# A transformer block's two layer norms: the inverse root as a power on GpSimd instead of a square root on ScalarE

## The reference

```
def _layernorm(x, axis=-1, eps=1e-05):
    m = jnp.mean(x, axis=axis, keepdims=True)
    v = jnp.var(x, axis=axis, keepdims=True)
    return (x - m) / jnp.sqrt(v + eps)

h = emb_weight[ids] + (lora_A[:, ids].T @ lora_B.T) * 2
h = h + attention(_layernorm(h))      # 16 heads of 16, window of 64 to each side, plus 64 global keys, gated
h = h + experts(_layernorm(h))        # 8 experts, 256 -> 1024 -> 256, the best 2 per token, capacity 1.25
```

## Time and profile before

| | us |
|---|---|
| timed runs | 3863.5, 3874.36, 3875.84 (median 3874.36) |
| span of the profiled execution, first to last instruction | 3869.2 |
| busy: TensorE, GpSimd, VectorE, ScalarE | 3468.8, 2331.8, 2237.8, 1988.5 |

### The profile page before, as it was taken

The page is one execution under the profiler, slowest core; times in us unless marked ns, Lnnn a source line. Parts: engine busy times, 40 slices in busy tenths (PEclk is TensorE's granted clock), DMA queues, the critical chain, the costliest instruction groups (busy, mean ns, idle before and its releaser), DMA issues. The chain is left out here.

```text
span 3869.2 us, 118995 instructions
## 1 busy us (share of the span) xinstructions
PE 3468.8 (90%) x47729; PEld 2822.7 (73%) x47730; DVE 2237.8 (58%) x5391; ACT 1988.5 (51%) x3119; POOL 2331.8 (60%) x2664
## 2 busy tenths in 40 slices
PE   3889898889998989988998759999999998999998
PEld 1566565656565656565655559999999998999998
DVE  3577777777777687777786433434333433343333
ACT  0566666666665666666666434444444444444343
POOL 5467768677777777777776544444444444444443
PEclk7899999999999999999999879999999999999999
DMA  4445445444544444444444132333333333222222
GB/s 138 128 149 150 139 129 158 130 151 132 154 135 147 133 146 142 146 138 150 140 149 131 55 98 46 66 49 59 57 57 58 59 56 67 47 50 45 44 45 40
DMA packets 242497, 397.77 MB, mean 103 GB/s; under 512 B 34572, under 2 KB 150748, under 8 KB 242044
## 3 DMA queue, kind: packets, MB, share of 16 engines
q1 hardware_dynamic: 168540, 297.43, 24.8%
q0 software_dynamic: 70512, 91.16, 13.6%
q10 hardware_dynamic: 3008, 2.95, 0.2%
HBM read 198.55 MB, written 192.88 MB: 101 GB/s over the span
## 5 line engine op out<-in xcount | busy, mean ns | idle before, releaser
L1349 POOL DMA_INDIRECT out_y<-out_t,tok_out x264 | 425.2, 1611 | 766.5 <-DMA out_y<-out_t,tok_out 390.3
L1495 ACT ACTIVATE act<-psS 128x512 f32<-128x512 f32 x528 | 316.2, 599 | 907.8 <-PE psS L1423 907.8
L1557 DVE TENSOR_TENSOR h_lo<-act,h_hi 128x512 fp32r<-128x512 f32 x528 | 367.1, 695 | 586.6 <-ACT h_hi L1496 586.6
L879 ACT ACTIVATE pl<-psS 128x896 f32<-128x896 f32 x512 | 468.5, 915 | 291.5 <-PE psS L727 285.0
L1458 PE MATMUL psO<-w_hi,h_hi 128*128 128x256 f32 x2112 | 598.5, 283 | 0.0
L1458 PE MATMUL psO<-w_lo,h_hi 128*128 128x256 f32 x2112 | 588.6, 279 | 0.0
L1458 PE MATMUL psO<-w_hi,h_lo 128*128 128x256 f32 x2112 | 587.6, 278 | 0.0
L556 POOL TENSOR_SCALAR_AFFINE_SELECT pl<-pl 128x512 f32<-128x512 f32 x512 | 353.3, 690 | 376.9 <-ACT pl L879 375.9
L1423 PE MATMUL psS<-xg_hi,w_hi 128*128 128x256 f32 x1984 | 551.8, 278 | 0.0
L1423 PE MATMUL psS<-xg_hi,w_lo 128*128 128x256 f32 x1984 | 551.5, 278 | 0.0
L1423 PE MATMUL psS<-xg_lo,w_hi 128*128 128x256 f32 x1984 | 551.4, 278 | 0.0
(11 more groups left out here) (233 smaller groups left out, 7780.4 us busy)
## 6 DMA issues: line engine op xcount, KB each, us to landing
qk_scr<-qk SPq DMA_DIRECT2D x64, 768.0 KB, 4.2
Q<-qk_scr SPq DMA_DIRECT2D x128, 384.0 KB, 4.5
K<-qk_scr SPq DMA_DIRECT2D x128, 384.0 KB, 5.3
qk_scr<-qk SPq DMA_DIRECT2D x64, 512.0 KB, 3.4
qk_scr<-qk SPq DMA_DIRECT2D x64, 256.0 KB, 3.4
h_rows<-held SPq DMA_DIRECT2D x32, 512.0 KB
hb<-h_rows SPq DMA_DIRECT2D x32, 512.0 KB
out_y<-h SPq DMA_DIRECT2D x32, 512.0 KB
```

What stands on the lines that cost most here:

```text
L879: act.activation(pl[:, v, half, :, lo:hi], psS[:, 0:2, lo:hi], ACT.Exp, scale=SCALE).then_inc(exp_done, 1)
L1349: pool.indirect_dma_start(out=y[:, :], in_=out_t[:, tile.out, s, :], in_offset=None, out_offset=bass.IndirectOffsetOnAxis(ap=tok_out[:, ti ...
L1495: act.activation(act32[:, b, :, 0:cols], src, ACT.Silu)
L1557: dve.tensor_tensor(h_lo[:, 2 * b:2 * b + 2, 0:cols], act32[:, b, :, 0:cols], h_hi[:, 2 * b:2 * b + 2, 0:cols].bitcast(F32), ALU.subtract) ...
```

## The change

The square roots on ScalarE go. VectorE adds epsilon to the variances (`var1`, `var2`), and GpSimd raises the sums to the power of minus one half, with a constant tile `neg_half` as the exponent; VectorE's reciprocals go as well. The new entries stand here in the lists: on VectorE `var2` behind the second half of `stats2`, `var1` behind the second half of `stats1`; on GpSimd `rstd2` between the selects of exponentials 12 and 13, and `rstd1` behind the last `residual` and ahead of the next sequence's first select. `scale2` of block 0 moves on VectorE from before `kg` 0 to behind the maximum 4. Nothing else is moved.

```
-                    dve.memset(eps_b[:, :], EPS)
+                    dve.memset(neg_half[:, :], -0.5)
 ORDER["act"]
-                ("cur", "exp", 11), ("cur", "exp", 12), ("prev", "std2", None), ("cur", "exp", 13), ...
+                ("cur", "exp", 11), ("cur", "exp", 12), ("cur", "exp", 13), ...
-                ("far", "std1", None), ("cur", "exp", 19), ...
+                ("cur", "exp", 19), ...
 ORDER["dve"]
-                ("nxt", "rstd1", None), ("cur", "cut", (1, 0)), ...
+                ("cur", "cut", (1, 0)), ...
-                ("far", "lora", 0), ("nxt", "max", 3), ("prev", "rstd2", None), ("prev", "scale2", 0), ("nxt", "kg", 0),
-                ("far", "lora", 1), ("nxt", "max", 4), ("prev", "scale2", 1), ...
+                ("prev", "var2", None), ("far", "lora", 0), ("nxt", "max", 3), ("nxt", "kg", 0),
+                ("far", "lora", 1), ("nxt", "max", 4), ("prev", "scale2", 0), ("prev", "scale2", 1), ...
-                ("nxt", "max", 8), ("far", "stats1", 1), ("nxt", "max", 9),
+                ("nxt", "max", 8), ("far", "stats1", 1), ("far", "var1", None), ("nxt", "max", 9),
 ORDER["pool"]
-                ("old", "scatter", 4), ("cur", "sel", 12), ("cur", "sel", 13), ("next", "gather", 0), ...
+                ("old", "scatter", 4), ("cur", "sel", 12), ("prev", "rstd2", None), ("cur", "sel", 13), ("next", "gather", 0), ...
-                ("cur", "sel", 18), ("prev", "residual", 2), ("prev", "residual", 3), ("nxt", "sel", 0), ...
+                ("cur", "sel", 18), ("prev", "residual", 2), ("prev", "residual", 3), ("far", "rstd1", None), ("nxt", "sel", 0), ...
 GpSimd
+                        if stage == "rstd1":
+                            pool.wait_ge(var1_done, s + 1)
+                            pool.tensor_tensor(rstd1[:, :], var1[:, :], neg_half[:, :], ALU.pow).then_inc(rstd1_done, 1)
 ScalarE
-                        if stage == "std1":
-                            act.wait_ge(mv1_done, s + 1)
-                            act.activation(std1[:, :], mv1[:, :, 1], ACT.Sqrt, bias=eps_b[:, :]).then_inc(std1_done, 1)
 VectorE
-                        if stage == "rstd1":
-                            dve.wait_ge(std1_done, s + 1)
-                            dve.reciprocal(rstd1[:, :], std1[:, :]).then_inc(rstd1_done, 1)
+                        if stage == "var1":
+                            dve.wait_ge(mv1_done, s + 1)
+                            dve.tensor_scalar(var1[:, :], mv1[:, :, 1], EPS, None, ALU.add).then_inc(var1_done, 1)
```

More of the change, by code:

```diff
@@ L144, in build @@
         neg_bg = keep("neg_bg", [P, 1])
-        eps_b = keep("eps_b", [P, 1])
+        neg_half = keep("neg_half", [P, QB])
         iota8 = keep("iota8", [P, E])
@@ L481, in build @@
                 ("cur", "exp", 9), ("far", "embed", None), ("cur", "exp", 10), ("cur", "evac", (1, 0)), ("nxt", "gate", None),
-                ("cur", "exp", 11), ("cur", "exp", 12), ("prev", "std2", None), ("cur", "exp", 13), ("cur", "evac", (1, 1)),
+                ("cur", "exp", 11), ("cur", "exp", 12), ("cur", "exp", 13), ("cur", "evac", (1, 1)),
                 ("cur", "exp", 14), ("cur", "exp", 15), ("nxt", "m_rows", 0), ("cur", "exp", 16), ("prev", "x2_t", 0),
                 ("prev", "x2_t", 1), ("cur", "exp", 17), ("cur", "exp", 18), ("cur", "evac", (2, 0)), ("cur", "evac", (2, 1)),
-                ("far", "std1", None), ("cur", "exp", 19), ("nxt", "values", 0), ("nxt", "values", 1), ("nxt", "m_rows", 1),
+                ("cur", "exp", 19), ("nxt", "values", 0), ("nxt", "values", 1), ("nxt", "m_rows", 1),
                 ("nxt", "values", 2), ("far", "xn_t", 0), ("far", "xn_t", 1), ("far", "qk", 0), ("nxt", "exp", 0),
@@ L489, in build @@
             ORDER["dve"] = (
-                ("nxt", "rstd1", None), ("cur", "cut", (1, 0)), ("cur", "kg", 1), ("cur", "cut", (1, 1)), ("old", "rank", 3),
+                ("cur", "cut", (1, 0)), ("cur", "kg", 1), ("cur", "cut", (1, 1)), ("old", "rank", 3),
                 ("nxt", "scale1", 0), ("cur", "cut", (1, 2)), ("cur", "gate1", None), ("cur", "kg", 2), ("cur", "cut", (1, 3)),
@@ L511, in build @@
                 ("cur", "sel", 8), ("nxt", "hold", 1), ("nxt", "hold", 2), ("nxt", "hold", 3), ("cur", "sel", 10), ("cur", "sel", 11),
-                ("old", "scatter", 4), ("cur", "sel", 12), ("cur", "sel", 13), ("next", "gather", 0), ("next", "gather", 1),
+                ("old", "scatter", 4), ("cur", "sel", 12), ("prev", "rstd2", None), ("cur", "sel", 13), ("next", "gather", 0), ("next", "gather", 1),
                 ("next", "gather", 2), ("old", "scatter", 5), ("old", "scatter", 6), ("old", "scatter", 7), ("cur", "sel", 15),
                 ("prev", "residual", 0), ("cur", "sel", 16), ("cur", "sel", 17), ("next", "gather", 3), ("prev", "residual", 1),
-                ("cur", "sel", 18), ("prev", "residual", 2), ("prev", "residual", 3), ("nxt", "sel", 0), ("far", "qk3", 0),
+                ("cur", "sel", 18), ("prev", "residual", 2), ("prev", "residual", 3), ("far", "rstd1", None), ("nxt", "sel", 0), ("far", "qk3", 0),
                 ("far", "qk3", 1), ("past", "scatter", 0), ("far", "qk3", 2), ("far", "qk3", 3), ("nxt", "sel", 1), ("nxt", "sel", 2),
@@ L596, in _ @@
                             pool.tensor_tensor(qk3[:, arg, :], qk_rest[:, arg, :], qk2[:, arg, :], ALU.subtract).then_inc(qk3_done, 1)
+                        if stage == "rstd1":
+                            pool.wait_ge(var1_done, s + 1)
+                            pool.tensor_tensor(rstd1[:, :], var1[:, :], neg_half[:, :], ALU.pow).then_inc(rstd1_done, 1)
+                        if stage == "rstd2":
+                            pool.wait_ge(var2_done, s + 1)
+                            pool.tensor_tensor(rstd2[:, :], var2[:, :], neg_half[:, :], ALU.pow).then_inc(rstd2_done, 1)
                         if stage == "hold":
@@ L1151, in _ @@
                             ins.then_inc(mv1_done, 1)
-                        if stage == "rstd2":
-                            dve.wait_ge(std2_done, s + 1)
-                            dve.reciprocal(rstd2[:, :], std2[:, :]).then_inc(rstd2_done, 1)
+                        if stage == "var2":
+                            dve.wait_ge(mv2_done, s + 1)
+                            dve.tensor_scalar(var2[:, :], mv2[:, :, 1], EPS, None, ALU.add).then_inc(var2_done, 1)
                         if stage == "scale2":
```

13 lines of the change are left out of this document (5 added, 8 removed).

## The result

The changed kernel takes 3923.89 us (median of 4 runs, 3922.38 to 3935.31) against 3875.1 us for the kernel before on the same chip (4 runs, 3863.5 to 3887.53): a ratio of 1.0131, 95% interval 1.0109 to 1.0152. It is 49 us slower. The forecast of 3890 us had the sign, and the time lies in its wide range, but 9 us above the forecast's own range of 3875 to 3915. The span went from 3869.2 us to 3922.8 us.

A forecast was written before the change was run, and what follows sets the result against it. Each turn was taken to run along GpSimd's burst up to `xn`: 0.2 us shorter, plus 0.6 us of clock falls, +0.4 us; 29 turns +12 us, ends +3.5 us, giving 3890 us (own range 3875 to 3915, wide 3848 to 3945).

The forecast's parts named there:

- What is removed: ScalarE's table loads and roots, 5.7 us a turn; TensorE's 1.73 us idle before L734 and GpSimd's 1.62 us wait go.
- The mechanism at `xn`: `xn` hangs on GpSimd's burst; `rstd1` behind the last residual adds X, 0.1 us handing over and 2.73 us of scales.
- forecast's sum: Per turn -1.62 + X + X + 0.1 + 2.73 - 2.4 = -1.2 + 2X; with clock falls +0.4 us.
- X: Length of one added GpSimd power, taken as 0.5 us; at 0.6 us nothing of the turn's gain is left.
- The price of a power: A 128x4 power on GpSimd takes 0.5 us, between a 187 ns copy and an upper end of 1155 ns.
- The turn until L837: TensorE's own work would reach L837 some 2.9 us earlier, but `xn` comes only 0.2 us earlier.
- The clock: TensorE idles before L755, `m_rows` and L837; a fall costs 1.6 us, in four turns of ten, 0.6 us a turn.
- VectorE's additions: Additions of epsilon replace 0.18 us reciprocals on VectorE; the exchange costs nothing, differing by hardly 0.1 us.
- The ends: First `xn` 3.4 us later as the pipeline fills; three scatters at the other end hidden by GpSimd's idle: +3.5 us.
- The rival in which the loads remain: Powers are added but ScalarE's loads stay for another function's sake: about 3915 us, chance 0.03.

The follow-up runs named there:

- rstd1_back: The changed kernel with the first norm's root back on ScalarE and VectorE's reciprocal, only `rstd2` a GpSimd power: 3795.81 us, ratio 0.9806 to the kernel before.
- the pair without the shut-out: The kernel before and the changed kernel, each with `top` 7 and 8 moved behind maxima 18 and 19 on VectorE: 3817.04 and 3844.01 us.

## Why the prediction came out as it did, point by point

- **What is removed: right.** The loads went from 130 to 2, L734's wait for ScalarE from 40.7 us to nothing, and the 1.62 us that GpSimd lost in its burst with it. The half of the change that does this, `rstd2`, is worth 30 us with the shut-out away, and 75 us in rstd1_back, where the shut-out and the clock fall better as well.
- **The mechanism at `xn`: right.** In nearly every turn `xn` is done 3.79 us after the last residual, which is the power, 0.01 us and the 2.73 us of the scales. The forecast's sum said X + 0.1 + 2.73.
- **The price of a power: the step that failed.** "A power of four elements a lane must cost more than an addition, so I take 0.5 us, nearer to the copy than to the 1155 ns which is my upper end." It took 1.05 us, near the upper end. The rows showed GpSimd at under 3 ns an element for arithmetic (747 ns for 256); the power's 159 ns was in none of them. With X = 1.05 the forecast's sum gives -1.2 + 2.1 + 0.6 = +1.5 us a turn, 29 turns and the ends +47 us, against +49 us measured. That closeness is partly luck, as the next points show.
- **The turn until L837: smaller than that sum.** The burst's end came 0.74 us earlier in the mean (38.19 to 37.45 us), where the sum with 1.05 us says 0.57, and L843 starts 0.58 us later than L837 did (0.67 us in the pair without the shut-out), not 0.9.
- **The clock: right for the place foreseen, which is the smaller part.** The lower clock stood behind L734's wait in 13 of the 26 turns before and stands behind L799's wait, on L843, in 11 after: the forecast's four in ten. But most of it follows the maxima, behind L707 in 14 turns before and behind L713 in 23 after. In all it covers 5.5 us of a turn after and 4.4 us before.
- **What was missed.** No term of the sum, and no rival, had the shut-out of VectorE's L1020, though the text had its 2406 ns in hand and set it aside: "the sum below does not need it". It grew by 1.11 us a turn, in front of a maximum that TensorE waits for; about half of the loss goes with it.
- **VectorE's additions: wrong in size, without a shown effect.** They "can hardly differ from it by 0.1 us"; the mean of `var1` is 1.68 us, 1.90 us where GpSimd's selects lie over it. With no select over it, as the pipeline fills, it takes 0.17 us. VectorE idles 1.72 us for the power behind it, so it is covered where it stands; that is argued from this wait, and no run left the addition out.
- **The ends: right when the pipeline fills.** The first scale of `xn` started at 74.37 us instead of 71.01, 3.36 us later; 3.4 was forecast.

```profile
74.37 1.38 DVE L1170 TENSOR_SCALAR xn<-h,mv,rstd 128x256 f32<-128x256 f32 x4 [4.35 <-POOL rstd L599]
```

When it empties, GpSimd still idles 2.67 us after the three scatters and the residuals, so they held nobody at the end.

The sum over turns is larger than the result: 26 times 2.31 us is 60 us, the span grew by 53.6 us. Of the turns in which the pipeline empties one is 4.5 us shorter than before and the next 2.4 us longer, and what comes behind them is 3.0 us shorter. Open is why L1020 waits 3.1 us in every turn with `rstd1`'s power and 1.2 or 2.4 us before. In the mean the first select starts 0.01 us ahead of L1020 before and 0.01 us behind it after, which by the order above goes with a longer wait. The gathers (L570) and mixes (L589) of GpSimd ahead of the selects take some 20 ns more in the median, enough for it, but what lengthens them was not tested. (The rival in which the loads remain adds up to 3918 us, not 3915; nothing hangs on it.)

## What to carry to other kernels

Before an operation is moved to another engine to spare a table load, measure it there at its own size: on GpSimd a power is paid by the element, 75 times a multiplication. Judge each half of a change by itself, since here one half wins and the other loses more than that, and the place decides: a power for which the next engine waits costs its length and the clock behind the idle, and two entries earlier it costs 24 us less. And a small VectorE instruction ahead of one on which TensorE depends should not be asked for as GpSimd begins a row of instructions; an entry or two earlier or later is worth 1.5 to 2% here.

## What the runs showed of the hardware that was not expected

- VectorE's L1020 (two bf16 inputs of 128x8 in SBUF, 0.1 us), asked for within some 0.04 us of the start of GpSimd's first select, is held for two selects (1.23 us), four (2.40 us), or four and a mix (3.10 us); 0.01 to 0.03 us decide, and on the whole the earlier request waits longer. Asked for 0.6 us ahead of the select, it passes; 0.14 or 0.40 us into one, it waits for the end of that one. A maximum out of PSUM runs through the same selects in 0.82 us. (The Trainium skill, SBUF — State Buffer, section on the two separate sides, says that the first to start holds the shared port pair for its whole instruction. The waits of 0.25 and 0.50 us agree, with one instruction each; near the start they do not: L1020 waited for a row of up to five instructions, in most turns of the changed kernel although its own record starts first, and the measurement decides.)
- A power on GpSimd takes about 0.4 us and 159 ns an element: 0.58 us for one, 1.00 us for four alone, 1.05 us for four in the loop, 10.5 us for 64.
- The kernel before, without any power, runs 1.5% faster when `top` 7 and 8 stand behind the maxima (3817.04 us), which is the same shut-out taken away.
